# Product matmuls and gate matmuls in turn, in a gated MLP on one Trainium2 core

## The chip, the core and the metric

The kernel runs on one core of a Trainium2 chip (trn2). The time is that of the device for one execution, in microseconds; what is shown is the median of three runs. TensorE (PE, with its weight loads as PEld), VectorE (DVE), ScalarE (ACT), GpSimd (POOL) and the DMA queue of SyncE (SP) run side by side and wait for each other by semaphores.

## What is computed

Four sequences of 512 tokens with 256 features go through two residual layers. The first is a 256x256 layer whose weights are mixed per sequence out of eight matrices. The second is a gated MLP: a shared one, and the best two of eight experts for the sequence.

```
def _gemma_mlp(x, gate_w, up_w, down_w):
    g = jnp.einsum('bsh,hi->bsi', x, gate_w)
    u = jnp.einsum('bsh,hi->bsi', x, up_w)
    return jnp.einsum('bsi,ih->bsh', jax.nn.gelu(g, approximate=True) * u, down_w)
...
x = x + _L0_cond_ref(x, cond_8, L0_cond_weight, L0_cond_mask, L0_cond_bias)
x = x + _L1_cond_ref(x, cond_8, ...)
```

## The kernel before, in words

Tokens lie along the free axis, features on the partitions. A sequence is a "batch" of 24 steps, eight for the shared MLP and eight for each of its two experts. Step s makes 128 of the hidden features for all 512 tokens: a **gate** projection into g_ps, an **up** projection into u_ps (two halves, used in turn), gelu on ACT (L740), the product h of both on DVE (L995 or L1000), and a **down** projection that accumulates over the steps. Every operand of a matmul is split into a rounded part (hi) and a rest (lo), and each product of matrices is three products of parts. Gate and up are thus six matmuls of 512 columns each (`project`, L501 to L509; matmuls at L504, L505, L508).

The down projection has two forms. In batch 0, and for the last four steps of the last batch, it is plain: six matmuls of 512 columns (L556, or L605 by halves). Elsewhere (`fast`) two steps make a pair p, and Winograd's variant of Strassen's method multiplies a 2x2 of blocks with seven products in place of eight. The right-hand blocks are halves of h of 256 tokens (B11, B21, B22) and sums of them (T1 to T4, formed by DVE, split by ACT and DVE); the left-hand ones are blocks of the down weights and sums S1 to S4. Each product is three matmuls of 256 columns (`product`, L561 to L564; matmul L563). After the even step of a pair come P1, P2 and P3 (nine matmuls, `products_123`), after the odd one P6, P7, P4 and P5 (twelve, `products_4567`). P1, P6 and P7 lie in p_ps, the others in o_ps, both in PSUM. The order on PE is written out by hand, with LAG = 2:

```
for s in range(STEPS):
    if s + LAG < STEPS:
        gate_up(b, s + LAG)
    ...
    down(b, s)
```

so PE runs gate(s+2), up(s+2), down(s), gate(s+3), and so on. Batches 1 and 2 are one loop on every engine. Twice in a batch six matmuls of the next batch's first layer follow a down (L463).

What PE waits for: a gate waits for the gelu before it to have read g_ps, and for the lo part of its weights (POOL, L1193); the gate of step 0 for the parts of the new x1 as well (POOL, L1244). A down waits for h_lo. ACT takes its work in a fixed order: gelu of a step (L740); after an even one the copy of T (L767) and, once DVE has h, that of B11 (L754), which waits until all nine matmuls of the pair before are done (`down_done`), then b12 (L757); after an odd one the copy of B21 and B22 (L762). Weight splits (L711, L720, L722) come between. At a batch's end ACT also empties the PSUM of the products (L772, L773 once P1 to P3 are through, L777, L778 once P4 to P7 are) before the next gelu.

Of the kernel before, what the change touches and what calls it, by code (L numbers as in the profile page):

```python
# [35 lines left out]
def build(nc, xT, cond, l0_w, l0_mask, experts, shared, outT):  # L36
# [22 lines left out]
    with ExitStack() as ctx:  # L59
# [6 lines left out]
        def sem(name):  # L66
            return ctx.enter_context(nc.semaphore(name))
# [118 lines left out]
        t_done = sem("t_done")  # L186
        t_hi_done = sem("t_hi_done")
        t_lo_done = sem("t_lo_done")
        down_done = sem("down_done")
        sum0_done = sem("sum0_done")  # L190
        evac_done = sem("evac_done")
# [19 lines left out]
        def at_first(b):  # L211
            return isinstance(b, int) and b == 0
# [47 lines left out]
        def pair_count(b, p):  # L260

            return NP * (b - 1) + p
# [158 lines left out]
        def _(pe):  # L421
# [54 lines left out]
            def block_of(w, i):  # L476
                return w[:, i * P:(i + 1) * P]

            def half_of(h, i):
                return h[:, i * TH:(i + 1) * TH]  # L480
# [30 lines left out]
            def gate_up(b, s):  # L511
                n = STEPS * b + s
                w_hi, w_lo = gu_weights(s)
# [12 lines left out]
                pe.wait_ge(gelu_done, n)  # L526
                project(g_ps, w_hi, w_lo, GATE, b).then_inc(g_done, 1)
                if by_parts:
                    pe.wait_ge(gu_hi_done, s + 1)
                    pe.wait_ge(gu_lo_done, s + 1)  # L530
                if s < 2 and not at_first(b):
                    was_fast = not (isinstance(b, int) and b == 1)
                else:
                    was_fast = fast(b, s // 2 - 1)
                if was_fast and s % 2:
                    pe.wait_ge(t_done, 4 * pair_count(b, s // 2 - 1) + 4)
                elif not isinstance(n, int) or n >= 2:
                    pe.wait_ge(h_lo_done, n - 1)
                project(u_ps[:, s % 2], w_hi, w_lo, UP, b).then_inc(u_done, 1)
# [18 lines left out]
                        mm.then_inc(sum0_done, 1)  # L558
                mm.then_inc(down_done, 1)

            def product(ps, wt, ht, blk, hf, first, last):  # L561
                for i, (w, h) in enumerate(((0, 0), (0, 1), (1, 0))):
                    mm = pe.matmul(ps, block_of(wt[w], blk), half_of((h_hi, h_lo)[h], hf), start=(first and i == 0), stop=(last and i == 2))  # L563
                return mm  # L564

            def products_123(b, p):
                wait_d(b, p)
                pe.wait_ge(h_lo_done, STEPS * b + 2 * p + 2)
                if p == 0:
                    pe.wait_ge(x1_done, HH)  # L570
                    pe.wait_ge(out_done, 1)
                    pe.wait_ge(evac_done, 4 * b)
                first, last = p == 0, p == (LAST_FAST - 1 if at_last(b) else NP - 1)
                wt = d_weights(p)
                product(P1, wt, None, A11, B11, first, last)
                product(P2, wt, None, A12, B21, first, False)
                product(P3, wt, None, S4, B22, False, last).then_inc(down_done, 1)

            def products_4567(b, p):
                pe.wait_ge(t_lo_done, pair_count(b, p) + 1)  # L580
                if p == 0:
                    pe.wait_ge(out_done, HH)
                    pe.wait_ge(evac_done, 4 * b + 2)
                    if not (isinstance(b, int) and b == 1):
                        pe.wait_ge(x1_p4_done, b - 1)
                first, last = p == 0, p == (LAST_FAST - 1 if at_last(b) else NP - 1)
                wt = d_weights(p)
                product(P6, wt, None, S2, T2, first, False)
                product(P7, wt, None, S3, T3, False, last)
                product(P4, wt, None, A22, T4, first, False)  # L590
                product(P5, wt, None, S1, T1, False, last).then_inc(down_done, 1)

            def final_down(s):
                wh, wl = d_weights(s // 2)
# [11 lines left out]
                    if s == STEPS - 1:  # L606
                        mm.then_inc(final_done, 1)

            def down(b, s):
                if fast(b, s // 2):  # L610
                    if s % 2 == 0:
                        products_123(b, s // 2)
                    else:
                        products_4567(b, s // 2)
                elif at_first(b):
                    plain_down(b, s, [o_ps[:, oh] for oh in range(HH)], s == 0, s == STEPS - 1)
                elif s < STEPS - FINAL:
                    pe.wait_ge(x1_done, HH * B)
                    pe.wait_ge(rest_done, 1)
                    plain_down(b, s, LAST_PS, True, True)  # L620
                else:
                    final_down(s)

            def batch(b, with_next):
                for s in range(STEPS):
                    if s + LAG < STEPS:
                        gate_up(b, s + LAG)
                    elif with_next:
                        gate_up(b + 1, s + LAG - STEPS)
                    down(b, s)  # L630
                    if with_next and s == 13:
                        first_layer(b + 1, 0)
                    if with_next and s == 16:
                        first_layer(b + 1, 1)


            def keep_warm(count):
                for _ in range(count):
# [16 lines left out]
                    keep_warm(1)  # L655
            first_layer_0()
            first_gate_up()
            gate_up(0, 1)
            batch(0, True)
            with pe.Fori(1, B - 1) as b:  # L660
                batch(b, True)
# [3 lines left out]
        def _(act):  # L665
# [84 lines left out]
            def split_b11(b, p):  # L750
                n = STEPS * b + 2 * p
                act.wait_ge(h_done, n + 1)
                act.wait_ge(down_done, n - 1)
                act.copy(h_hi[:, 0:TH], u_ps[:, 0, 0:TH]).then_inc(h_hi_done, 1)  # L754
                if not (isinstance(b, int) and b == 1 and p == 0):
                    act.wait_ge(t_done, 4 * pair_count(b, p))
                act.copy(b12[:], u_ps[:, 0, TH:T]).then_inc(b12_done, 1)  # L757

            def split_b2(b, p):
                n = STEPS * b + 2 * p + 1  # L760
                act.wait_ge(h_done, n + 1)
                act.copy(h_hi[:, B21 * TH:(B22 + 1) * TH], u_ps[:, 1]).then_inc(h_hi_done, 1)  # L762

            def split_t(b, p):
# [595 lines left out]
```

## Time and profile before

| | |
|---|---|
| median of 3 runs | 416.71 us (415.83 to 416.97) |
| profiled execution | 416.73 us |
| its span (first to last instruction) | 414.9 us |
| PE busy | 409.4 us, 2133 matmuls |
| PE weight loads busy | 350.6 us, 2133 loads |
| DVE, ACT, POOL busy | 262.1, 234.7, 256.7 us |
| DMA | 36.24 MB, mean 87 GB/s |

A matmul's row in the profile starts where it starts streaming, and its length includes the way through the array, so that rows of neighbouring matmuls overlap. What a matmul costs is the distance from its start to the next one's. A row "x2" merges two instructions. "Idle before" counts only time in which the engine had nothing at all.

### The profile page before, as it was taken

To read this page: it belongs to the slowest core of one execution; us is meant where nothing else is said; L and a number is where in the kernel's file an instruction comes from. 1 tells how busy PE (TensorE), PEld (TensorE's weight loads), DVE (VectorE), ACT (ScalarE), POOL (GpSimd) and SP (SyncE) were. 2 spreads that over 40 slices of the span, in tenths; PEclk is the share of its full clock that TensorE was granted. 3 is DMA by queue.
4 is the path that set the end of the run, shared out by engine and by line. 5 is a ranking of instruction groups with operands and counts; after the bars stand their busy time and mean duration, and the time that the engine had idled before them with its cause. 6 is when DMAs were issued, how large, how long until landed. Compare 5 with 4: busy or idle time off the path is not lost.

```text
span 414.9 us, 7010 instructions
## 1 busy us (share of the span) xinstructions
PE 409.4 (99%) x2133; PEld 350.6 (85%) x2133; DVE 262.1 (63%) x452; ACT 234.7 (57%) x448; POOL 256.7 (62%) x275
## 2 busy tenths in 40 slices
PE   8999999999999999999999999999999999999997
PEld 5688888888888888888888888888888888888886
DVE  3556644244348877865767878775666675666684
ACT  5665454463425567665556566666465555766541
POOL 1565465378702459988533878998560885878630
DMA  7764324334200442243110053322300033222101
GB/s 241 244 199 108 96 81 126 98 102 104 76 25 9 122 126 76 77 134 96 42 38 0 25 177 90 112 76 76 101 25 25 0 117 87 78 92 87 40 12 51
DMA packets 20187, 36.24 MB, mean 87 GB/s; under 512 B 2242, under 2 KB 3010, under 8 KB 20162
## 3 DMA queue, kind: packets, MB, share of 16 engines
q1 hardware_dynamic: 19872, 35.66, 28.5%
q8 instruction: 13, 0.21, 0.2%
q10 hardware_dynamic: 290, 0.26, 0.2%
q14 instruction: 12, 0.10, 0.1%
HBM read 33.82 MB, written 2.10 MB: 87 GB/s over the span
## 4 chain that ended last, share of the span: by engine, by line
PE 96%; DMA 1%; DVE 1%; SPq 1%; issue 0%; ACT 0%; DVEq 0%
PE o_ps L563 12%; PE g_ps L505 11%; PE g_ps L504 11%; PE g_ps L508 10%; PE u_ps L505 10%; PE u_ps L508 10%; PE u_ps L504 10%; PE p_ps L563 9%; PE o_ps L556 8%; PE l_ps L463 2%; DMA l_raw<-l_w 1%; PE p_ps L444 1%; DVE t_raw L941 0%; PE o_ps L605 0%; SPq L276 0%
## 5 line engine op out<-in xcount | busy, mean ns | idle before, releaser
L1193 POOL TENSOR_TENSOR eg_lo<-raw_g,eg_hi 128x512 fp32r<-128x512 f32 x64 | 85.8, 1356 | 41.2 <-ACT eg_hi L711 41.2
L1000 DVE SCALAR_TENSOR_TENSOR u_ps<-gelu,route_cur,u_ps 128x512 f32<-128x512 f32 x64 | 48.3, 754 | 77.0 <-PE u_ps L508 77.0
L740 ACT ACTIVATE gelu<-g_ps 128x512 f32<-128x512 f32 x96 | 57.7, 601 | 59.7 <-PE g_ps L508 59.1
L505 PE MATMUL g_ps<-x_hi,eg_lo 128*128 128x512 f32 (+1 forms) x128 | 50.4, 394 | 0.0
L504 PE MATMUL g_ps<-x_hi,eg_hi 128*128 128x512 f32 (+1 forms) x128 | 50.1, 392 | 0.0
L505 PE MATMUL u_ps<-x_hi,eg_lo 128*128 128x512 f32 (+1 forms) x128 | 49.8, 389 | 0.0
L504 PE MATMUL u_ps<-x_hi,eg_hi 128*128 128x512 f32 (+1 forms) x128 | 49.8, 389 | 0.0
L762 ACT CAST h_hi<-u_ps 128x512 fp32r<-128x512 f32 x34 | 19.9, 587 | 49.8 <-DVE u_ps L1000 31.1
L1036 DVE TENSOR_TENSOR h_lo<-t_raw,h_hi 128x1024 fp32r<-128x1024 f32 x34 | 47.3, 1392 | 0.0
L995 DVE TENSOR_TENSOR u_ps<-gelu,u_ps 128x512 f32<-128x512 f32 x32 | 22.3, 696 | 31.2 <-PE u_ps L508 30.2
L1232 POOL TENSOR_TENSOR ed_lo<-raw_d,ed_hi 128x384 fp32r<-128x384 f32 x22 | 22.4, 1020 | 30.2 <-ACT ed_hi L720 30.2
L508 PE MATMUL g_ps<-x_lo,eg_hi 128*128 128x512 f32 (+1 forms) x128 | 39.6, 390 | 0.0
L508 PE MATMUL u_ps<-x_lo,eg_hi 128*128 128x512 f32 (+1 forms) x128 | 39.4, 389 | 0.0
L711 ACT CAST eg_hi<-raw_g 128x512 fp32r<-128x512 f32 x64 | 37.2, 621 | 0.0
L767 ACT CAST h_hi<-t_raw 128x1024 fp32r<-128x1024 f32 x34 | 35.6, 1048 | 0.3
L1031 DVE TENSOR_TENSOR h_lo<-u_ps,h_hi 128x512 fp32r<-128x512 f32 x34 | 23.5, 691 | 17.0 <-ACT h_hi L762 17.0
L754 ACT CAST h_hi<-u_ps 128x256 fp32r<-128x256 f32 x34 | 12.7, 373 | 32.9 <-PE o_ps L563 30.8
L1236 POOL TENSOR_TENSOR ed_lo<-raw_d,ed_hi 128x512 fp32r<-128x512 f32 x10 | 13.9, 1394 | 27.1 <-ACT ed_hi L724 27.1
L508 PEld LDWEIGHTS g_ps<-x_lo,eg_hi 128*128 128x128 f32 x128 | 24.0, 188 | 5.3
L504 PEld LDWEIGHTS u_ps<-x_hi,eg_hi 128*128 128x128 f32 x128 | 24.0, 188 | 5.2
L1234 POOL TENSOR_TENSOR ed_lo<-s_raw,ed_hi 128x512 fp32r<-128x512 f32 x22 | 28.4, 1290 | 0.0
L505 PEld LDWEIGHTS u_ps<-x_hi,eg_lo 128*128 128x128 f32 x128 | 24.0, 188 | 5.0
(234 smaller groups left out, 1120.6 us busy)
## 6 DMA issues: line engine op xcount, KB each, us to landing
raw_g<-experts SPq DMA_DIRECT2D x64, 256.0 KB, 2.8
raw_d<-experts SPq DMA_DIRECT2D x32, 256.0 KB, 2.8
l_raw<-l_w SPq DMA_DIRECT2D x8, 256.0 KB, 5.7
x_in<-xT SPq DMA_DIRECT2D x8, 256.0 KB, 4.4
raw_g<-shared SPq DMA_DIRECT2D x8, 256.0 KB, 4.4
raw_d<-shared SPq DMA_DIRECT2D x8, 256.0 KB, 2.9
outT<-out_sb SPq DMA_DIRECT2D x6, 256.0 KB, 3.2
mask<-l_mask SPq DMA_DIRECT2D x2, 128.5 KB, 6.0
```

Of the source, the lines that this page charges most:

```text
L504: pe.matmul(ps, w_hi[:, at:at + P], x1_at(x1_hi, b, hh), start=(hh == 0), stop=False)
L505: pe.matmul(ps, w_lo[:, at:at + P], x1_at(x1_hi, b, hh), start=False, stop=False)
L508: mm = pe.matmul(ps, w_hi[:, at:at + P], x1_at(x1_lo, b, hh), start=False, stop=(hh == HH - 1))
L556: mm = pe.matmul(psums[oh], block_of(w, blk), x, start=(first and i == 0), stop=(last and i == 2))
L563: mm = pe.matmul(ps, block_of(wt[w], blk), half_of((h_hi, h_lo)[h], hf), start=(first and i == 0), stop=(last and i == 2))
L711: act.copy(eg_hi[:, j % RING], raw_g[:, j % RAW_G]).then_inc(gu_hi_done, 1)
L740: act.activation(gelu[:, s % 2], g_ps[:], ACT.Gelu_apprx_tanh).then_inc(gelu_done, 1)
L767: act.copy(h_hi[:, T1 * TH:7 * TH], t_raw[:]).then_inc(t_hi_done, 1)
L1000: dve.scalar_tensor_tensor(u_ps[:, s % 2], gelu[:, s % 2], route_cur[:, k:k + 1], u_ps[:, s % 2], ALU.mult, ALU.mult).then_inc(h_done, 1)
L1036: dve.tensor_tensor(h_lo[:, at], t_raw[:], h_hi[:, at].bitcast(F32), ALU.subtract).then_inc(t_lo_done, 1)
L1193: pool.tensor_tensor(eg_lo[:, j % RING], raw_g[:, j % RAW_G], eg_hi[:, j % RING].bitcast(F32), ALU.subtract).then_inc(gu_lo_done, 1)
L1234: pool.tensor_tensor(ed_lo[:, q % RING_D, S1 * P:7 * P], s_raw[:], ed_hi[:, q % RING_D, S1 * P:7 * P].bitcast(F32), ALU.subtract).then_inc ...
```

## The change

PE's order is rotated: a step is now up(s+2), then down(s) with gate(s+3) laid into it. Gate matmuls, each for itself, alternate with the product matmuls of `fast` pairs; where the down is plain, the gate follows it as before. The matmuls are the same, 2133 of them. In the even step P1's three come first, then the waits of the gate, then gate and product in turn; in the odd step the gate's waits come after four products. P1's last matmul counts a new semaphore, `b11_read`, and ACT's copy of B11 waits for that (its three readers) and no longer for P2 and P3. The copy of B21 and B22 gets the wait that it had through B11's: `down_done` at n - 2.

```
             def up(b, s):
...
-            def products_123(b, p):
+            def products_123_and_gate(b, p, nb, ns):
+
                 wait_d(b, p)
                 pe.wait_ge(h_lo_done, STEPS * b + 2 * p + 2)
...
-                product(P1, wt, None, A11, B11, first, last)
-                product(P2, wt, None, A12, B21, first, False)
-                product(P3, wt, None, S4, B22, False, last).then_inc(down_done, 1)
...
+                product(P1, wt, A11, B11, first, last).then_inc(b11_read, 1)
+                wait_gate(nb, ns)
+                gate_part(nb, ns, 0)
+                product_part(P2, wt, A12, B21, 0, first, False)
+                gate_part(nb, ns, 1)
+                product_part(P2, wt, A12, B21, 1, first, False)
+                gate_part(nb, ns, 2)
+                product_part(P2, wt, A12, B21, 2, first, False)
+                gate_part(nb, ns, 3)
+                product_part(P3, wt, S4, B22, 0, False, last)
+                gate_part(nb, ns, 4)
+                product_part(P3, wt, S4, B22, 1, False, last)
+                product_part(P3, wt, S4, B22, 2, False, last).then_inc(down_done, 1)
+                gate_part(nb, ns, 5).then_inc(g_done, 1)
...
-                product(P6, wt, None, S2, T2, first, False)
-                product(P7, wt, None, S3, T3, False, last)
-                product(P4, wt, None, A22, T4, first, False)
-                product(P5, wt, None, S1, T1, False, last).then_inc(down_done, 1)
+                product(P6, wt, S2, T2, first, False)
+                product_part(P7, wt, S3, T3, 0, False, last)
+                wait_gate(nb, ns)
+                gate_part(nb, ns, 0)
+                product_part(P7, wt, S3, T3, 1, False, last)
+                product_part(P7, wt, S3, T3, 2, False, last)
+                gate_part(nb, ns, 1)
+                product_part(P4, wt, A22, T4, 0, first, False)
+                product_part(P4, wt, A22, T4, 1, first, False)
+                gate_part(nb, ns, 2)
+                product_part(P4, wt, A22, T4, 2, first, False)
+                product_part(P5, wt, S1, T1, 0, False, last)
+                gate_part(nb, ns, 3)
+                product_part(P5, wt, S1, T1, 1, False, last)
+                gate_part(nb, ns, 4)
+                product_part(P5, wt, S1, T1, 2, False, last).then_inc(down_done, 1)
+                gate_part(nb, ns, 5).then_inc(g_done, 1)
...
             def batch(b, with_next):
                 for s in range(STEPS):
                     if s + LAG < STEPS:
-                        gate_up(b, s + LAG)
+                        up(b, s + LAG)
                     elif with_next:
-                        gate_up(b + 1, s + LAG - STEPS)
-                    down(b, s)
+                        up(b + 1, s + LAG - STEPS)
+                    if s + LAG + 1 < STEPS:
+                        down_and_gate(b, s, b, s + LAG + 1)
+                    elif with_next:
+                        down_and_gate(b, s, b + 1, s + LAG + 1 - STEPS)
+                    else:
+                        down_and_gate(b, s, None, None)
...
             def split_b11(b, p):
                 n = STEPS * b + 2 * p
                 act.wait_ge(h_done, n + 1)
-                act.wait_ge(down_done, n - 1)
+                if p == 0:
+                    act.wait_ge(down_done, n - 1)
+                else:
+                    act.wait_ge(b11_read, pair_count(b, p))
...
             def split_b2(b, p):
                 n = STEPS * b + 2 * p + 1
                 act.wait_ge(h_done, n + 1)
+                act.wait_ge(down_done, n - 2)
```

PE in the loop over batches, before: a down of an even step, between the up of one step and the gate of the next. The weights are sd_hi and sd_lo for the down, sg_hi and sg_lo for gate and up.

```order
L508 MATMUL u_ps<-x_lo,sg_hi 128x512 x2
L563 MATMUL p_ps<-h_hi,sd_hi 128x256
L563 MATMUL p_ps<-h_lo,sd_hi 128x256
L563 MATMUL p_ps<-h_hi,sd_lo 128x256
L563 MATMUL o_ps<-h_hi,sd_hi 128x256
L563 MATMUL o_ps<-h_lo,sd_hi 128x256
L563 MATMUL o_ps<-h_hi,sd_lo 128x256
```

Three more o_ps matmuls and the six of the gate follow. The same place in the changed kernel:

```order
L579 MATMUL p_ps<-h_hi,sd_hi 128x256
L579 MATMUL p_ps<-h_lo,sd_hi 128x256
L579 MATMUL p_ps<-h_hi,sd_lo 128x256
L525 REGISTER_ALU
L533 MATMUL g_ps<-x_hi,sg_hi 128x512
L579 MATMUL o_ps<-h_hi,sd_hi 128x256
L533 MATMUL g_ps<-x_hi,sg_lo 128x512
L579 MATMUL o_ps<-h_lo,sd_hi 128x256
L533 MATMUL g_ps<-x_hi,sg_hi 128x512
L579 MATMUL o_ps<-h_hi,sd_lo 128x256
```

The gate's matmuls stand between those of P2 and P3, and the register instruction of the gate's wait stands in the middle of the down instead of behind it.

ACT in the loop, before: the copies of T and B11, and the work behind them.

```order
L767 CAST h_hi<-t_raw 128x1024 [waits down_done,t_done]
L754 CAST h_hi<-u_ps 128x256 [waits down_done,h_done]
L756 ISA
L757 COPY b<-u_ps 128x256 [waits t_done]
L716 ISA
```

And in the changed kernel:

```order
L826 CAST h_hi<-t_raw 128x1024 [waits down_done,t_done]
L811 REGISTER_ALU [waits h_done]
L812 CAST h_hi<-u_ps 128x256 [waits b11_read]
L814 REGISTER_ALU
L815 COPY b<-u_ps 128x256 [waits t_done]
```

Nothing moves on ACT; the copy of B11 waits for b11_read in place of down_done.

## Rows read from the trace of the kernel before

**Rows 1.** The page: span and busy time by engine.
```profile
span 414.9 us, 7010 instructions
...
PE 409.4 (99%) x2133; PEld 350.6 (85%) x2133; DVE 262.1 (63%) x452; ACT 234.7 (57%) x448; POOL 256.7 (62%) x275
```
**Rows 2.** The page: chain that ended last, by engine.
```profile
PE 96%; DMA 1%; DVE 1%; SPq 1%; issue 0%; ACT 0%; DVEq 0%
```
**Rows 3.** Timeline of PE, batch 1 (start us, length us, engine, line, operation): even step, odd down.
```profile
200.68 0.28 PE L563 MATMUL p_ps<-h_hi,ed_hi 128*128 128x256 f32 x1
200.79 0.28 PE L563 MATMUL p_ps<-h_lo,ed_hi 128*128 128x256 f32 x1
...
201.75 0.40 PE L504 MATMUL g_ps<-x_hi,eg_hi 128*128 x1
201.99 0.40 PE L505 MATMUL g_ps<-x_hi,eg_lo 128*128 x1
202.22 0.39 PE L504 MATMUL g_ps<-x_hi,eg_hi 128*128 x1
...
203.14 0.39 PE L504 MATMUL u_ps<-x_hi,eg_hi 128*128 x1
...
204.50 0.28 PE L563 MATMUL p_ps<-h_hi,ed_hi 128*128 128x256 f32 x1
204.61 0.28 PE L563 MATMUL p_ps<-h_lo,ed_hi 128*128 128x256 f32 x1
204.73 0.28 PE L563 MATMUL p_ps<-h_hi,ed_lo 128*128 128x256 f32 x1
...
205.93 0.40 PE L504 MATMUL g_ps<-x_hi,eg_hi 128*128 x1
```
**Rows 4.** Timeline of PE, batch 0: gate, up and plain down.
```profile
67.20 0.39 PE L504 MATMUL g_ps<-x_hi,eg_hi 128*128 128x512 f32 x1
...
68.56 0.39 PE L504 MATMUL u_ps<-x_hi,eg_hi 128*128 128x512 f32 x1
...
71.28 0.39 PE L504 MATMUL g_ps<-x_hi,eg_hi 128*128 128x512 f32 x1
```
**Rows 5.** Timeline of PE weight loads, at the second product block of Rows 3.
```profile
204.50 0.19 PEld L563 LDWEIGHTS p_ps<-h_lo,ed_hi 128*128 128x128 f32 x1
204.62 0.19 PEld L563 LDWEIGHTS p_ps<-h_hi,ed_lo 128*128 128x128 f32 x1
```
**Rows 6.** Line L563: length in ns min/median/max of the first product matmul and the next.
```profile
L563 PE MATMUL p_ps<-h_hi,ed_hi x66: 277/278/284, 158.0 to 399.6; 128*128 128x256 f32 x66
...
L563 PE MATMUL p_ps<-h_lo,ed_hi x66: 282/283/284, 158.1 to 399.7; 128*128 128x256 f32 x66
...
L563 PE MATMUL p_ps<-h_hi,sd_hi x36: 277/278/381, 125.9 to 351.6; 128*128 128x256 f32 x36
```
**Rows 7.** Who waited for whom: PE's longest since batch 0, and ACT's before L754.
```profile
PE g_ps L504 <- ACT gelu L740: 0.3, 1, 0.3
ACT h_hi L754 <- PE o_ps L563: 30.8, 33, 1.2
```
**Rows 8.** Timelines of ACT and PE: gelu of step 9 and gate 10, batch 1.
```profile
153.28 0.61 ACT L740 ACTIVATE gelu<-g_ps 128x512 f32<-128x512 f32 x1
155.21 0.40 PE L504 MATMUL g_ps<-x_hi,eg_hi 128*128 x1
```
**Rows 9.** Timeline of ACT at the end of batch 1.
```profile
218.49 0.39 ACT L772 COPY x_in<-p_ps 128x256 f32<-128x256 f32 x1
218.75 0.62 ACT L773 COPY s_raw<-o_ps 128x512 f32<-128x512 f32 x1
219.34 0.60 ACT L740 ACTIVATE gelu<-g_ps 128x512 f32<-128x512 f32 x1
```
**Rows 10.** Timelines of POOL and PE: lo weights of gates 8 and 9, gate 8, batch 3.
```profile
332.74 3.54 POOL L1193 TENSOR_TENSOR eg_lo<-raw_g,eg_hi 128x512 fp32r<-128x512 f32 x2
344.65 0.40 PE L504 MATMUL g_ps<-x_hi,eg_hi 128*128 128x512 f32 x1
```

More of the change, by code:

```diff
@@ L188, in build @@
         t_lo_done = sem("t_lo_done")
+        b11_read = sem("b11_read")
         down_done = sem("down_done")
@@ L509, in project, with wait_gate @@
                 return mm
-            def gate_up(b, s):
-                n = STEPS * b + s
-                w_hi, w_lo = gu_weights(s)
+            def wait_gate(b, s):
                 by_parts = at_first(b) and s < FIRST
@@ L525, in gate_up, with gate_part, gate, up @@
                     pe.wait_ge(x1_lo_done, HH * b + HH)
-                pe.wait_ge(gelu_done, n)
-                project(g_ps, w_hi, w_lo, GATE, b).then_inc(g_done, 1)
-                if by_parts:
+                pe.wait_ge(gelu_done, STEPS * b + s)
+            def gate_part(b, s, i):
+                w_hi, w_lo = gu_weights(s)
+                hh = i // 2 if i < 4 else i - 4
+                w, x = (w_lo if i in (1, 3) else w_hi), (x1_hi if i < 4 else x1_lo)
+                at = GATE + hh * P
+                return pe.matmul(g_ps, w[:, at:at + P], x1_at(x, b, hh), start=(i == 0), stop=(i == 5))
+            def gate(b, s):
+                wait_gate(b, s)
+                for i in range(6):
+                    mm = gate_part(b, s, i)
+                mm.then_inc(g_done, 1)
+            def up(b, s):
+                n = STEPS * b + s
+                w_hi, w_lo = gu_weights(s)
+                if at_first(b) and s < FIRST:
                     pe.wait_ge(gu_hi_done, s + 1)
@@ L559, in plain_down, with product_part, product @@
                 mm.then_inc(down_done, 1)
-            def product(ps, wt, ht, blk, hf, first, last):
-                for i, (w, h) in enumerate(((0, 0), (0, 1), (1, 0))):
-                    mm = pe.matmul(ps, block_of(wt[w], blk), half_of((h_hi, h_lo)[h], hf), start=(first and i == 0), stop=(last and i == 2))
+            def product_part(ps, wt, blk, hf, i, first, last):
+                w, h = ((0, 0), (0, 1), (1, 0))[i]
+                return pe.matmul(ps, block_of(wt[w], blk), half_of((h_hi, h_lo)[h], hf), start=(first and i == 0), stop=(last and i == 2))
+            def product(ps, wt, blk, hf, first, last):
+                for i in range(3):
+                    mm = product_part(ps, wt, blk, hf, i, first, last)
                 return mm
-            def products_123(b, p):
+            def products_123_and_gate(b, p, nb, ns):
                 wait_d(b, p)
@@ L574, in products_123, with products_4567_and_gate @@
                 wt = d_weights(p)
-                product(P1, wt, None, A11, B11, first, last)
-                product(P2, wt, None, A12, B21, first, False)
-                product(P3, wt, None, S4, B22, False, last).then_inc(down_done, 1)
-            def products_4567(b, p):
+                product(P1, wt, A11, B11, first, last).then_inc(b11_read, 1)
[12 more added lines that the diff above has]
+                gate_part(nb, ns, 5).then_inc(g_done, 1)
+            def products_4567_and_gate(b, p, nb, ns):
                 pe.wait_ge(t_lo_done, pair_count(b, p) + 1)
@@ L607, in final_down, with down_and_gate @@
                         mm.then_inc(final_done, 1)
-            def down(b, s):
+            def down_and_gate(b, s, nb, ns):
                 if fast(b, s // 2):
                     if s % 2 == 0:
-                        products_123(b, s // 2)
+                        products_123_and_gate(b, s // 2, nb, ns)
                     else:
-                        products_4567(b, s // 2)
-                elif at_first(b):
+                        products_4567_and_gate(b, s // 2, nb, ns)
+                    return
+                if at_first(b):
                     plain_down(b, s, [o_ps[:, oh] for oh in range(HH)], s == 0, s == STEPS - 1)
@@ L622, in down @@
                     final_down(s)
+                if ns is not None:
+                    gate(nb, ns)
             def batch(b, with_next):
@@ L657, in _ @@
             first_gate_up()
-            gate_up(0, 1)
+            gate(0, 1)
+            up(0, 1)
+            gate(0, 2)
             batch(0, True)
```

## The prediction

> **What bounds the kernel now.** I read the page first. PE is busy 409.4 of 414.9 us [rows 1], and the chain that ended last is PE for 96% [rows 2]; the list of waits has PE idle for 0.3 us at most once the first gate has run [rows 7]. So no wait is worth anything by itself: the time is the number of matmuls times the distance from one start to the next. The timelines of PE give that distance, and it isn't the same everywhere.
>
> - **512 columns behind 512.** Batch 0 has nothing else: eighteen matmuls from gate to gate in 71.28 - 67.20 = 4.08 us [rows 4], 0.227 each. Six are 1.36 us.
> - **256 columns in a block.** Nine products and the first gate matmul: 201.75 - 200.68 = 1.07. Eight of the distances, from 200.79 on, are 0.96, so 0.120 each, and the first is 0.11. Twelve: 205.93 - 204.50 = 1.43, of which the first is again 0.11 [rows 3]. The record of the first product is 278 ns long, of the second 283, in p_ps at every one of some hundred places [rows 6]. I take 0.113 for a product that stands directly behind a 512, 0.120 for one behind another product.
> - **512 behind a block.** The six gate matmuls after nine products take 203.14 - 201.75 = 1.39, the up behind them 204.50 - 203.14 = 1.36 [rows 3], and in batch 0 gate is 1.36 as well [rows 4]. A block leaves 0.03 us to be paid by those that follow it, the first two most (0.24 and 0.23).
>
> Every load starts at the start of the matmul before its own: loads at 204.50, 204.62 [rows 5] against matmuls at 204.50 and 204.61 [rows 3]. So one load is under way per matmul and no more. Behind a 512 it has 0.227 us; in a block load follows load at 0.12, and its 0.19 us reach past the start of the matmul that uses it. The clock granted was 2.4 GHz, at which 256 columns alone are 0.107 us.
>
> **The change, part by part.** Its worth is counted over `fast` steps: p_ps's first matmuls number 66 + 36 = 102 at L563 [rows 6], three a pair, so 34 pairs, 68 steps.
>
> *Products between gate matmuls.* Nothing is added to or taken from PE's matmuls; only neighbours change. Even step: behind an up or a gate matmul stand P1's first, three of P2, P3's first and P3's second, six at 0.113; three stay behind a product. Before, one was short and eight long. Five more are shorter by 0.007, that is 0.035 us. Odd step: P6's first, P7's second, P4's first and third, P5's second and third are short, six again, where it was one: 0.035. Together 68 x 0.035 = 2.4 us.
>
> *The debt of a block.* 0.03 for 68 steps is 2.0 us in all. It may vanish, since no run of more than four products is left; or stay, since the gate's first matmul still stands behind three or four products, and nine leave the same debt as twelve would, so its size doesn't grow with the block. The trace has no shorter block. The ends are 2.0 us gained and nothing; below nothing, it may be paid again after every product, which is the third rival. I take nothing: the nearest row, a gate matmul behind a product, is the 0.24 at 201.75 [rows 3].
>
> *Loads of the page.* The Trainium skill (TensorE: Matmul & The Clock Gate, LDWEIGHTS and Back-to-back issue gap) gives a load of 128 columns as 128 / 1.2, 107 ns, and a matmul as N / 2.4 + 2.5, 109 ns at 256. By it a load fits under a 256 as it does under a 512, a block costs nothing, and the sum would be zero. The 0.120 in place of 0.109 speaks against that, the equally unexplained 0.227 in place of 0.216 for it.
>
> *The gate's waits, moved forward.* They stand six products (0.72 us) earlier in the even step, eight (0.96) in the odd one, and now hold up products too. The gelu that gate 10 needs ended at 153.28 + 0.61 = 153.89, the gate began at 155.21 [rows 8]: 1.32 of slack, 0.36 after the move. Weights are no matter: those of gate 8 and 9 of batch 3 were there at 332.74 + 3.54 = 336.28, eight us before the gate at 344.65 [rows 10]. The register instruction in front of the wait stands in the middle of products; before, it stood behind twelve of them, and the distance to the gate was still 0.12. Nothing for all of it, by that cover.
>
> *Later ends of the downs.* P3 and P5 now end just before the gate does, some 1.1 us later against the gelu. Behind them on ACT is only the emptying of PSUM at a batch's end: 218.49 to 219.34, 0.85 us, and then the gelu, 0.60 [rows 9]. The gelu would end some 1.25 us after its gate; the next gate begins 1.36 (up) less 0.16 (the tail of the gate's record) plus 0.35 or 0.47 (products) after it, 1.55 or more. About 0.3 us are left, four times in the run. Nothing, again.
>
> *ACT's copy of B11.* ACT waited 30.8 us in 33 places for the products [rows 7], 0.93 each, with nobody behind it that held PE up. Left with `down_done` it would wait longer now; with `b11_read` it is free about a gate earlier. No time of its own, but it is what keeps ACT in step.
>
> **Sum.** 2.4 us less. Made against the profiled execution, 416.73 us (span 414.9 and 1.8 around it), which is the median of 416.71 too: **414.3 us**, 0.6% faster.
>
> **Rivals.**
> 1. *The debt goes as well.* 2.4 + 2.0 = 4.4 us: 412.3. For it: the first gate in batch 0, behind 512s, has no debt at all [rows 4], and with a 512 after every one or two products loads are never behind for long. Against it: the block of three or four.
> 2. *No gain.* What a short product saves, the next gate matmul gives back: the 0.007 at the head of a block would be a shift in when a record starts and no time. Five returned a step, 0.035, leave 416.7. For it: 0.24 for the first gate matmul is more than 0.007 over 0.227. It is also what the page's figures give. Against: the debt is 0.03 a block, not 0.007.
> 3. *Slower: the debt is paid after every product.* Each gate matmul stays at 0.235, as the first ones behind a block [rows 3], none recovers between products, the products find no head start and stay at 0.120, and the 0.03 moves on into the up. Even step with up: 9 x 0.12 + 6 x 0.235 + 1.39 = 3.88, before 1.07 + 1.39 + 1.36 = 3.82. 0.06 a step, 4.1 us: 420.8. It decides from where the gate and up matmuls of a step average over 0.232 with short products (3.82 less 1.038, by twelve).
> 4. *The gate finds gelu late.* The 0.3 and 0.36 us above hold only if ACT isn't later than by my count. 0.3 late at a dozen steps with the least slack is 3.6 us and eats the gain: about 418.
>
> **How the numbers follow.** Forecast 0.38, debt gone 0.28, no gain 0.19, slower by the debt 0.12, gelu late 0.03. What can be told from no change is 0.3%, 1.25 us. Forecast and first rival are beyond it: faster 0.66. No gain is within: same 0.19. The other two: slower 0.15. The range starts below the first rival, at 412.0, takes in no gain and part of the fourth, and ends at 417.4; the third is left out.
>
> **What would show it.** Products directly behind a gate matmul at 0.11 to the next start, gate matmuls between them at 0.227 to 0.24, the six distances of gate together some 1.39 (1.36: first rival; 1.41: third). A pair of steps (even 1.07, odd 1.43, and twice 1.39 + 1.36) 7.93 us where it is 8.00. No row in PE's waits for gelu over 0.1 us, and ACT's wait for L563 before the copy of B11 gone or far below 30.8 us. Wrong would be: PE waiting in the middle of a down, or gate matmuls that on average are over 0.235.

## The result, and the profile after

The changed kernel takes 418.45 us in the median (418.25 to 418.96, five runs), the kernel before 416.62 in the same comparison: a ratio of 1.005, 95% interval 1.0037 to 1.0064. It is slower by 0.5%, 1.8 us; forecast were 414.3 us and at most 417.4. The profiled execution took 418.25 us.

The page of the changed kernel: span, busy time, the chain that ended last by engine.

```profile
span 416.2 us, 7042 instructions
...
PE 411.3 (99%) x2133; PEld 350.8 (84%) x2133; DVE 263.4 (63%) x452; ACT 235.5 (57%) x448; POOL 256.3 (62%) x275
...
PE 94%; DVE 2%; DMA 1%; issue 1%; SPq 1%; ACT 1%; DVEq 0%
```

Against [rows 1, 2], PE is busy 1.9 us longer with the same 2133 matmuls. The chain that ended last is still PE, for 94%. Part of the loss is in what a matmul costs, part in waits. The timeline of PE in the changed kernel (start, length, engine, line, operation) shows where, in the even step that answers to the first block of [rows 3]:

```profile
200.28 0.28 PE L579 MATMUL p_ps<-h_hi,ed_hi 128*128 128x256 f32 x1
200.39 0.28 PE L579 MATMUL p_ps<-h_lo,ed_hi 128*128 128x256 f32 x1
...
200.63 0.40 PE L533 MATMUL g_ps<-x_hi,eg_hi 128*128 x1
200.86 0.28 PE L579 MATMUL o_ps<-h_hi,ed_hi 128*128 128x256 f32 x1
200.98 0.40 PE L533 MATMUL g_ps<-x_hi,eg_lo 128*128 x1
201.22 0.28 PE L579 MATMUL o_ps<-h_lo,ed_hi 128*128 128x256 f32 x1
201.34 0.40 PE L533 MATMUL g_ps<-x_hi,eg_hi 128*128 x1
201.58 0.28 PE L579 MATMUL o_ps<-h_hi,ed_lo 128*128 128x256 f32 x1
201.69 0.40 PE L533 MATMUL g_ps<-x_hi,eg_lo 128*128 x1
201.92 0.28 PE L579 MATMUL o_ps<-h_hi,ed_hi 128*128 128x256 f32 x1
202.04 0.40 PE L533 MATMUL g_ps<-x_lo,eg_hi 128*128 x1
...
202.52 0.40 PE L533 MATMUL g_ps<-x_lo,eg_hi 128*128 x1
202.76 0.40 PE L505 MATMUL u_ps<-x_hi,eg_hi 128*128 x1
...
204.12 0.28 PE L579 MATMUL p_ps<-h_hi,ed_hi 128*128 128x256 f32 x1
...
208.32 0.28 PE L579 MATMUL p_ps<-h_hi,ed_hi 128*128 128x256 f32 x1
```

The six gate distances are 0.23, 0.24, 0.24, 0.23, 0.24, 0.24, together 1.42 us where they were 1.39; the nine product distances are the rest of 202.76 - 200.28 = 2.48, so 1.06 where they were 1.07. Of the five products behind a gate matmul four take 0.12 to the next start and one (201.58) 0.11. A pair of steps is 208.32 - 200.28 = 8.04, before 8.00 (3.82 + 4.18). Over 34 pairs that is 1.36 us.

Two other losses are plain waits. The timelines of PE and of ACT at the start of batch 2:

```profile
220.56 0.28 PE L579 MATMUL p_ps<-h_hi,ed_hi 128*128 128x256 f32 x1
220.77 0.50 PE L533 MATMUL g_ps<-x_hi,sg_hi 128*128 x1
221.11 0.28 PE L579 MATMUL p_ps<-h_lo,ed_hi 128*128 128x256 f32 x1
```
```profile
218.80 0.37 ACT L812 CAST h_hi<-u_ps 128x256 fp32r<-128x256 f32 x1 [2.07 <-PE o_ps L579]
...
219.33 0.39 ACT L831 COPY x_in<-p_ps 128x256 f32<-128x256 f32 x1
...
220.08 0.64 ACT L795 ACTIVATE gelu<-g_ps 128x512 f32<-128x512 f32 x1
```

The gelu ends at 220.72 and the gate begins at 220.77; the two distances 0.21 and 0.34 stand for 0.12 and 0.23, and the step is 0.17 us longer. Ahead of that gelu ACT has not only the emptying of PSUM but the copies of B11 and b12, for B11's copy of a batch's *first* pair still waits for `down_done` and sat 2.07 us. The same happens at the start of batch 3: 0.33 us together. And the timeline of PE at the end:

```profile
411.18 0.28 PE L650 MATMUL g_ps<-l_hi,ed_lo 128*128 128x256 f32 x1
411.63 0.35 PE L650 MATMUL o_ps<-x_hi,ed_hi 128*128 128x256 f32 x1 [0.18 <-DVE x_lo L1065]
```

0.45 us where 0.12 is usual: 0.33 us for DVE, which sums the products behind the last fast pair, and got them late. In all 1.36 + 0.33 + 0.33 = 2.0 us, against 1.8 measured. The spans are only 1.3 us apart because the first gate began at different times, 19.48 us before and 18.75 after. From there to the start of the last matmul (411.67 and 413.01) it is 392.19 and 394.26, 2.1 us more, which fits the sum.

### The profile page after: what moved, and what is told of

Its sections match the earlier page's. It is cut to its first block, busy times and chain, and to the rows that moved or that the text cites. A ratio compares the mean times of both kernels' runs of the same rounds, so it can differ in the third digit from the quotient of the medians.

```text
span 416.2 us, 7042 instructions
## 1 busy us (share of the span) xinstructions
PE 411.3 (99%) x2133; PEld 350.8 (84%) x2133; DVE 263.4 (63%) x452; ACT 235.5 (57%) x448; POOL 256.3 (62%) x275
## 4 chain that ended last, share of the span: by engine, by line
PE 94%; DVE 2%; DMA 1%; issue 1%; SPq 1%; ACT 1%; DVEq 0%
PE g_ps L533 32%; PE o_ps L579 12%; PE u_ps L505 10%; PE u_ps L509 10%; PE u_ps L506 10%; PE p_ps L579 9%; PE o_ps L572 8%; PE l_ps L464 2%; DMA l_raw<-l_w 1%; PE p_ps L445 1%; DVE t_raw L1000 0%; SPq L277 0%; DVE u_ps L1059 0%; DVE out_sb L1144 0%; DVE x_lo L1065 0%
## 5 line engine op out<-in xcount | busy, mean ns | idle before, releaser
L1095 DVE TENSOR_TENSOR h_lo<-t_raw,h_hi 128x1024 fp32r<-128x1024 f32 x34 | 48.5, 1428 | 0.0
L533 PE MATMUL g_ps<-x_lo,eg_hi 128*128 128x512 f32 (+1 forms) x128 | 46.6, 395 | 0.0
L1291 POOL TENSOR_TENSOR ed_lo<-raw_d,ed_hi 128x384 fp32r<-128x384 f32 x22 | 24.1, 1093 | 30.6 <-ACT ed_hi L775 30.4
L509 PEld LDWEIGHTS u_ps<-x_lo,eg_hi 128*128 128x128 f32 x128 | 24.0, 188 | 5.0
```

The source lines that it names most:

```text
L533: return pe.matmul(g_ps, w[:, at:at + P], x1_at(x, b, hh), start=(i == 0), stop=(i == 5))
L1095: dve.tensor_tensor(h_lo[:, at], t_raw[:], h_hi[:, at].bitcast(F32), ALU.subtract).then_inc(t_lo_done, 1)
```

## The experiments

There are fourteen kernels. The table has those that settle what unequal lengths cost, each with a pair of steps in its profile (from one P1 to the next). The timeline resolves a hundredth of a microsecond, the time some tenths of a per cent. A *return* is a place where a matmul of 512 columns stands behind one of 256.

| kernel | a pair, us | returns from 256 to 512 columns in a pair | time, ratio to before |
|---|---|---|---|
| before | 8.00 | 2 | 1 |
| the change | 8.04 | 12 | 1.005 |
| e2 waits alone | 8.00 | 2 | 0.9997 |
| e10 gate in one piece | 8.04 | 4 | one run, 418.07 us |
| e11 two products a gate in even steps | 8.03 | 10 | one run, 417.77 us |
| e12 one product within up | 8.01 | 3 | one run, 417.65 us |
| e13, e14 one block of 21 | 7.98 | 1 | 1.0023, 1.0006 |

### The two parts of the change, and the two waits

**e1_b11_batch_start.**

```
             def split_b11(b, p):
-                if p == 0:
+                if isinstance(b, int) and b == 1 and p == 0:
                     act.wait_ge(down_done, n - 1)
```

> The changed kernel, with the copy of B11 of a batch's first pair (batches 2 and 3) also waiting for b11_read in place of down_done. Theory 1 (three separate costs in the profile of the change: 0.04 us in each of 34 pairs on PE, 0.165 us in front of the gate of step 3 at two batch starts, about 0.34 us in the last six steps): the two 0.165 us go, PE's distance at the first gate matmul of step 3 falls from 0.34 to 0.23, the pairs stay at 8.04 us; 0.33 us less than the change, 1.0035 to 1.0045 of before. Rival (ACT is late there because of emptying PSUM, not of the B11 copy): the 0.165 us stay and so does the time.

418.63 us, 1.0052 (1.0039 to 1.0064). The wait is gone, in the timeline of PE at the same place:

```profile
220.75 0.40 PE L533 MATMUL g_ps<-x_hi,sg_hi 128*128 x1
220.98 0.28 PE L579 MATMUL p_ps<-h_lo,ed_hi 128*128 128x256 f32 x1
```

and pairs stay at 8.04. The time doesn't show it: 0.33 us is a third of what the interval covers (1.0 us). The cause of the wait is shown, its 0.33 us in the profile alone.

**e2_wait_only.** The kernel before with the semaphores of the change, and `b11_read` for every pair but the very first:

```
-                product(P1, wt, None, A11, B11, first, last)
+                product(P1, wt, None, A11, B11, first, last).then_inc(b11_read, 1)
...
-                act.wait_ge(down_done, n - 1)
+                if isinstance(b, int) and b == 1 and p == 0:
+                    act.wait_ge(down_done, n - 1)
+                else:
+                    act.wait_ge(b11_read, pair_count(b, p))
```

> The kernel before with the new waits alone (b11_read for the copy of B11, down_done for that of B21 and B22), PE's order as before. Theory 1: PE waits for nothing there, so no difference: 1.000 of before, pairs at 8.00 us; ACT's 30.8 us of waiting in front of the B11 copy fall to under 20 us. Rival (the earlier copy of B11 collides with PE's reads or delays DVE): 0.04 us a pair, 1.003 or more.

416.64 us, 0.9997 (0.9988 to 1.0006), every pair 8.00. In front of the copy of B11 (L758 here) ACT waits 14.9 us in 22 places and 7.3 in 11 for DVE's product, 22.2 us instead of 30.8 for PE; the expected "under 20" is missed. It is idle time either way.

**e3_interleave_only.** The change, with B11 as before:

```
-                if p == 0:
-                    act.wait_ge(down_done, n - 1)
-                else:
-                    act.wait_ge(b11_read, pair_count(b, p))
+                act.wait_ge(down_done, n - 1)
```

> The changed kernel with the copy of B11 waiting for down_done as before, so the interleaving alone. Theory 1: the downs end 0.2 us before the gate does, so the B11 copy, b12 and on even steps from 8 the two weight copies (0.27 + 0.26 + 0.42 + 0.5 us) stand between the gate and the next gelu; with gelu's 0.6 that is about 1.84 us after the gate, where 1.67 are to be had: some 0.2 us lost at eight steps a batch, 4 us in all over the change, about 1.013 of before. Rival (ACT has room enough and the second part of the change is idle): same as the change, 1.0045.

429.64 us in the median of three runs (428.99 to 429.94), 1.0316 (1.0298 to 1.0334): 13 us over before, where 5 or 6 were expected. A fourth run took 1052.61 us, for a reason that isn't known, and is left out. PE was dry for 6.2 us before 21 gates, waiting for gelu. ACT's timeline at a step with a split of x:

```profile
160.83 0.37 ACT L809 CAST h_hi<-u_ps 128x256 fp32r<-128x256 f32 x1 [2.05 <-PE o_ps L579]
...
162.82 0.61 ACT L795 ACTIVATE gelu<-g_ps 128x512 f32<-128x512 f32 x1
```

The direction and the mechanism hold: two microseconds of copies between the end of the down and the gelu. The size was off, because at steps 8 and 10 the split of x stands there as well (the gate 0.95 us behind the product ahead of it), and because a late gate costs more than the delay of its gelu. Without that split, as at the gate of 171.94, the distance to the gate is 0.43 in place of 0.12 and the one behind it 0.34 in place of 0.23: 0.4 us, where 0.2 were expected. So the second part of the change isn't idle. It takes back some 11 us that the first would cost.

**e4_last_step_block.** e1, with the last fast step as before:

```
+                    elif at_last(b) and s == 2 * LAST_FAST - 1:
+                        products_4567(b, s // 2)
+                        gate(nb, ns)
```

> As e1_b11_batch_start, with the products of the last fast step in one block and gate 22 behind them, as in the kernel before. Theory 1: the sums of the products that DVE does at the end start 1.1 us earlier against the gate and the wait of 0.34 us in front of the last step's products goes: 0.3 us less than e1, about 1.003 of before, and what is left is the 0.04 us a pair (1.36 us, 1.0033). Rival (the wait at the end has another cause, the later gelu): no difference from e1.

417.98 us, 1.0031 (1.0019 to 1.0043), as expected (1.003); behind the start of batch 1 no distance over 0.25 us is left in its profile. With both waits gone, what remains is the 0.04 us a pair.

### What the unequal lengths cost

**e5_plain_alternate.** Batch 0's six down matmuls, all of 512 columns, in turn with the gate's.

```
+                        mm = pe.matmul(o_ps[:, oh], block_of(w, blk), x, ...)
...
+                        gm = gate_part(nb, ns, k)
```

> The changed kernel, and in batch 0 the six plain down matmuls of 512 columns (o_ps) alternate with the six of the gate (g_ps), 512 beside 512. Theory A (it is the unequal length that costs: a 512 behind a 256 takes 0.233 to 0.241 us to the next start): all distances in batch 0 stay at 0.227 and a step at 4.08 us. Theory B (it is the change of the PSUM tile or of the moving operand from one matmul to the next): distances of 0.233 or more in batch 0, a step of 4.12 us or more.

Theory A holds. PE in batch 0, from a down matmul to that of the next step:

```profile
62.29 0.39 PE L587 MATMUL o_ps<-h_hi,ed_hi 128*128 128x512 f32 x1
...
66.37 0.39 PE L587 MATMUL o_ps<-h_hi,ed_hi 128*128 128x512 f32 x1
```

4.08 us, 0.227 for each of eighteen. Neither the change of PSUM tile nor that of the moving operand costs anything. (Its one time, 419.5 against 417.08, isn't used: its first gate begins at 19.83, 1.1 us later than in the change.)

**e6_block_192 and e7_interleaved_192.** 192 columns in each product matmul, in blocks and interleaved:

```
-                    mm = pe.matmul(ps, block_of(wt[w], blk), half_of((h_hi, h_lo)[h], hf), ...)
+                    mm = pe.matmul(ps[:, 0:192], block_of(wt[w], blk), half_of((h_hi, h_lo)[h], hf)[:, 0:192], ...)
```

> The kernel before with product matmuls of 192 columns in place of 256, in blocks; the last 64 tokens of each half are left out of the products. Theory A (a product in a block is held at 0.12 us by its weight load, one load at a time): distances stay at 0.12 us, the time falls by nothing to speak of, and the 0.03 us debt of a block stays or grows. Theory B (0.12 is 256 columns at 2.4 GHz plus 0.013): 192 columns take 0.080 + 0.013, 0.093 us, 714 products give 19 us less.

> The changed kernel with product matmuls of 192 columns; the last 64 tokens of each half are left out of the products. Theory A (load bound): a product directly behind a gate matmul still takes 0.11 to 0.12 us to the next start, since the gate's load needs that; the gate matmuls behind take more than 0.24 us; not faster than e6. Theory B (length bound): products 0.093, gate matmuls as in the change, 0.233 to 0.241.

410.76 and 413.55 us in one run each, against 417.08 before: 6.3 and 3.5 less, not 19. PE and its loads in e6's block, then PE in e7:

```profile
195.01 0.28 PE L563 MATMUL p_ps<-h_hi,ed_lo 128*128 128x192 f32 x1
195.12 0.27 PE L563 MATMUL p_ps<-h_hi,ed_hi 128*128 128x192 f32 x1
...
196.12 0.41 PE L504 MATMUL g_ps<-x_hi,eg_hi 128*128 x1
```
```profile
195.03 0.19 PEld L563 LDWEIGHTS p_ps<-h_hi,ed_hi 128*128 128x128 f32 x1
195.14 0.19 PEld L563 LDWEIGHTS p_ps<-h_lo,ed_hi 128*128 128x128 f32 x1
```
```profile
200.17 0.25 PE L579 MATMUL o_ps<-h_hi,ed_hi 128*128 128x192 f32 x1
200.25 0.42 PE L533 MATMUL g_ps<-x_hi,eg_lo 128*128 x1
200.51 0.25 PE L579 MATMUL o_ps<-h_lo,ed_hi 128*128 128x192 f32 x1
```

In the block, loads and matmuls are 0.11 us apart, though interleaved products of this length show 0.08: this fits a bound by the load, and shorter products bring little. Interleaved, a product takes 0.08 to the next start, but the gate matmul behind it 0.26: together 0.34, as much as 0.11 and 0.227 apart. What the short product gives, the long one behind it gives back. This is theory A for e6, with 0.11 in place of 0.12, and for e7 except that the product itself is short. At 256 columns the loads could be 0.11 us apart but are 0.12 [rows 5], so there the load alone doesn't bound.

**e8_block_bf16.** Products of the upper halves of the same words, read as bf16 at a stride of two:

```
+ block_of(wt[w], blk).bitcast(BF16)[:, 1:2*P:2], half_of((h_hi, h_lo)[h], hf).bitcast(BF16)[:, 1:2*TH:2]
```

> The kernel before with the product matmuls' operands read as the upper halves (bf16) of the same words, 128 and 256 elements at a stride of two, in blocks; the products are of lower precision. Theory A (the load of four-byte weights is what holds a block at 0.12 us): distances fall to 0.107 to 0.113 us and the gate behind the block is at 0.227, 1.36 us for six; 21 x 0.01 + 0.06 us a pair, 9 us less. Theory B (a fixed cost for each pair of load and matmul): 0.12 us stays, and the debt as well.

414.32 us in one run. PE from P6 to the up:

```profile
203.44 0.29 PE L564 MATMUL p_ps<-h_hi,ed_hi 128*128 128x256 bf16 x1
...
204.70 0.28 PE L564 MATMUL o_ps<-h_hi,ed_lo 128*128 128x256 bf16 x1
204.72 0.48 PE L505 MATMUL g_ps<-x_hi,eg_hi 128*128 x1
205.04 0.40 PE L506 MATMUL g_ps<-x_hi,eg_lo 128*128 x1
...
207.58 0.29 PE L564 MATMUL p_ps<-h_hi,ed_hi 128*128 128x256 bf16 x1
```

and its first load of the block:

```profile
203.44 0.10 PEld L564 LDWEIGHTS p_ps<-h_hi,ed_hi 128*128 128x128 bf16 x1 [0.26 <-issue]
```

Neither theory holds whole. Ten of the twelve distances are 0.113, so the four-byte operands do hold a product at 0.12; whether the stationary or the moving one does it, this run can't tell. The first is 0.13. The gate's first matmul is recorded 0.02 behind the last product and then takes 0.32, together what 0.11 and 0.23 make, so the two records have to be taken together. The step is 207.58 - 203.44 = 4.14 us where it was 4.18, and twelve times 0.007 alone would give 0.08. So a block costs more here, 0.06 us in place of 0.02 (4.14 less 12 x 0.113 and 12 x 0.227). The debt is larger, not gone. The whole is 2.8 us less, not 9.

### Counting the returns

**e10_gate_in_one_piece.** On e4; the gate stands whole behind P1, or behind the first four products:

```
                 product(P1, wt, A11, B11, first, last).then_inc(b11_read, 1)
+                gate(nb, ns)
+                product(P2, wt, A12, B21, first, False)
+                product(P3, wt, S4, B22, False, last).then_inc(down_done, 1)
```

> As e4_last_step_block, but the gate laid in as one piece of six (even step: three products, gate, six products, up; odd step: four, gate, eight, up). Theory 1 (a cost for each return from products to 512): two returns of 0.02 us a step in place of one, even step 3.84, odd 4.20, a pair 8.04, the same as the full interleaving. Rival (only alternation one by one costs; long pieces are free): 8.00 as before.

```profile
201.12 0.40 PE L533 MATMUL g_ps<-x_hi,eg_hi 128*128 x1
...
202.51 0.28 PE L579 MATMUL o_ps<-h_hi,ed_hi 128*128 128x256 f32 x1
...
203.22 0.40 PE L505 MATMUL u_ps<-x_hi,eg_hi 128*128 x1
...
204.61 0.28 PE L579 MATMUL p_ps<-h_hi,ed_hi 128*128 128x256 f32 x1
```

The pair is 8.04 us (200.77 to 208.81). The gate behind three products takes 202.51 - 201.12 = 1.39, the up behind six 204.61 - 203.22 = 1.39: four returns in place of two cost 0.04 us, 0.02 each, with no single alternation at all. The rival falls.

**e11_two_products_a_gate.** On e4; in even steps `gate, product, product` three times, then three gate matmuls.

> As e4_last_step_block, but in even steps two products follow each of the first three gate matmuls and the last three gate matmuls are in a row: four returns from products to 512 in place of six. Theory 1: an even step loses 0.005 to 0.008 us for each return, 3.83 to 3.84, against 3.845 in the change and 3.82 before. Rival (the position of single products decides): no difference from e4, 3.845.

The pair is 8.03 us, between before and the change, as theory 1 has it. Seven pairs, from 208.92 to 265.11, are 56.19 us, 8.027 each, so ten returns cost 0.027 over before.

**e12_single_in_up.** On e2; P1's first matmul stands alone behind the up's third:

```
                     pe.matmul(ps, w_hi[:, at:at + P], x1_at(x1_hi, b, hh), start=(hh == 0), stop=False)
+                    if hh == 1 and between:
+                        between()
```

> The kernel e2_wait_only with the first product matmul of P1 (256 columns) standing alone between the third and fourth matmul of the up in front of it. Theory 1 (a 256 leaves the following 512 a distance of 0.233 or more even when it stands alone): the product 0.113, the 512 behind it 0.233, so together 0.346 as 0.120 + 0.227, even step 3.82 to 3.83. Rival (a single product behind several 512s costs 0.113 and leaves no debt): the 512 behind it 0.227, even step 3.81.

```profile
200.55 0.28 PE L576 MATMUL p_ps<-h_hi,ed_hi 128*128 128x256 f32 x1
200.66 0.40 PE L508 MATMUL u_ps<-x_hi,eg_lo 128*128 x1
...
201.36 0.28 PE L583 MATMUL p_ps<-h_lo,ed_hi 128*128 128x256 f32 x1
```

The plainest case of the question. The product itself takes 0.11, then the three matmuls of 512 columns behind it 201.36 - 200.66 = 0.70 where three are 0.68. So it gained 0.007 and lost nearly 0.02; the pair is 8.01. One single product behind 512s already leaves a debt, if a smaller one than a block that is followed by a whole gate.

**e9_one_block_of_21, e13_block_of_21_gelu_first, e14_block_of_21_tidied.** The law turned round: both downs of a pair behind each other, one return a pair. On e2:

```
+                    if fast(b, s // 2):
+                        if s % 2:
+                            down(b, s - 1)
+                            down(b, s)
+                    else:
+                        down(b, s)
```

> The kernel e2_wait_only with the two downs of a fast pair behind each other (up, nine products, twelve products, gate), so one block of 21 products a pair in place of two. Theory 1 (each return from products to 512 columns costs 0.02 us net, 0.027 paid by the matmuls behind less 0.007 at the head of the block, whatever the block's length): a pair takes 7.98 where it was 8.00, 34 x 0.02 = 0.7 us less, 0.998 of before, if ACT's next gelu is in time (B11, b12, weight copies and gelu behind P1, some 2.4 us, against 2.5 us of products). Rival (the debt grows with the length of the block): 8.00 or more. Second rival (gelu late at steps with x splits): PE stalls there, slower than before.

430.33 us, 1.0323 (1.0309 to 1.0337): PE stalls for late gelus, as the second rival has it, but before some 35 gates and not only at steps with splits of x. PE in batch 1:

```profile
164.99 0.50 PE L505 MATMUL g_ps<-x_hi,eg_hi 128*128 x1 [0.53 <-ACT gelu L746]
```

The gelu of the odd step stands on ACT behind the copy of B11, which now waits for a P1 that comes a gate and an up later. e13 puts that gelu ahead of the copy:

```
+                if not (s % 2 and fast(b, s // 2)):
+                    activate(b, s)
...
+                if s % 2 == 0 and fast(b, s // 2):
+                    activate(b, s + 1)
```

> As e9_one_block_of_21, with ACT's gelu of the odd step moved in front of the copy of B11, so that it no longer stands behind a copy that waits for the first three products. Theory 1 (a return from products to 512 columns costs 0.02 us, and e9's time was lost to late gelus alone): pairs of 7.98 us, no wait of PE for gelu over 0.1 us in the loop, 0.7 us less than before, 0.998. Rival (the gate of an odd step, which now follows its up directly, still finds gelu late because of the copies and splits ACT has ahead of it): stalls of 0.3 to 0.8 us at some steps stay and eat the 0.7 us.

417.61 us, 1.0023 (1.0014 to 1.0032). Two P1, a pair apart:

```profile
195.42 0.28 PE L564 MATMUL p_ps<-h_hi,ed_hi 128*128 128x256 f32 x1
...
203.40 0.28 PE L564 MATMUL p_ps<-h_hi,ed_hi 128*128 128x256 f32 x1
```

7.98 us: a block of 21 leaves the same debt as one of nine, and one return fewer gives 0.02 back. Both expectations are met at once, for four late gelus and a wait at the end cost more than that. e14 mends three places: `pick_cond` at step 2 ahead of B11, the splits of x at steps 7 and 8, the last fast pair in two blocks.

> As e13_block_of_21_gelu_first, with the three places mended where it waited: the small copy of the mixing weights at step 2 stands on ACT before the copy of B11 and not behind it, the two splits of the next x stand at steps 7 and 8 in place of 8 and 10, and the last fast pair has its products in two blocks as before. Theory 1 (0.02 us for each return from products to 512 columns, nothing else): 33 pairs x 0.02 = 0.66 us less than before, 0.9984, no wait for gelu over 0.1 us. Rival (each mended wait only lets the next one show, or the 0.02 us come back elsewhere): 1.000 or more.

417.01 us, 1.0006 (0.9996 to 1.0015). The end is as before and the wait of step 5's gate is gone, but the gate of step 13 still waits some 0.2 us and that of step 9 now 0.3, in batches 1 and 2. That is the rival's first half. Five pairs of batch 3 stay at 8.00, and there the trace shows something new. PE at one of their gates, then its loads:

```profile
371.61 0.40 PE L505 MATMUL g_ps<-x_hi,eg_hi 128*128 128x512 f32 x1
...
372.99 0.39 PE L505 MATMUL u_ps<-x_hi,eg_hi 128*128 128x512 f32 x1
```
```profile
371.16 0.19 PEld L509 LDWEIGHTS u_ps<-x_lo,eg_hi 128*128 128x128 f32 x1
371.40 0.19 PEld L505 LDWEIGHTS g_ps<-x_hi,eg_hi 128*128 128x128 f32 x1
```

In these pairs the gelu ended 0.10 us or less ahead of the last matmul of the up (behind those that end 0.16 or more ahead nothing is lost), and the gate's load started late by 0.02 us (four times) or 0.07 (once): here 0.24 behind the load before it in place of 0.23. PE was never dry, and there are only 512s around, yet some 0.02 us are lost at each, here 372.99 - 371.61 = 1.38 for a gate of 1.36, with a first distance of 0.24, like that of a gate behind a block. The lateness of the load alone doesn't settle it, since the load of the gate at 347.62 was 0.05 late and cost nothing. Had all 33 pairs kept their 0.02 us the gain would be 0.7 us, less than the width of its interval (0.8). No version that computes the same result beat the kernel before.

## Why the prediction was wrong

**The bound** was read right: PE, by the number of matmuls times their distances, and no wait. The list of distances was right too; 0.227, 0.120, 0.113 and the debt of 0.03 us come back in every kernel whose blocks are of 256 columns in fp32r.

**Products between gate matmuls, 2.4 us, with the debt taken as nothing: the step that failed.** It took 0.113 for the worth of every product behind a 512 and let the debt stay as it was, one a step. Both halves were off. Of six products a step that were to take 0.113 two do (in the even step those at 200.28 and 201.58), so the nine are 1.06 and not 1.04. And the debt grew, where the sum had no change and its bounds only a gain of 2.0 us or nothing. Over a pair, by the starts in both timelines, the 21 products take 2.48 us where they took 2.51 (0.026 less; 0.07 less was forecast), and the 24 matmuls of 512 columns 5.56 where they took 5.49 (0.065 more; no change was forecast): in 34 pairs 0.9 us less and 2.2 more. The two terms together came to +1.4 us in place of -2.4, of the wrong sign.

The reason that they can't be booked apart is in e12: its lone product gained 0.007 and its three followers paid nearly 0.02. In fp32r a short distance at a block's head and long ones behind the block came together in every kernel. Counted by returns, the law reads: a pair of steps is 21 x 0.120 + 24 x 0.2267 = 7.96 us, and 0.02 net for each return that is followed by six or more matmuls of 512 columns, 7.98 with one (e13), 8.00 with two, 8.04 with four (e10). A return that is cut off by the next product costs less: 12 returns cost 0.04 over 2.

**The third rival** came true in its mechanism, the debt beginning anew behind each product, at a third of its price: 0.04 a pair for 0.12. Its gate, 1.41, was right (1.42); but the products kept a part of their short distances (1.06 and not 1.08), and the up behind them was 204.12 - 202.76 = 1.36, not 1.39. Its threshold fits: the gate and up matmuls of the even step average (1.42 + 1.36) / 12 = 0.232, right at it, and with products longer than its 1.038 the step is 3.84, over 3.82. It had a chance of 0.12, and the range left it out. The trace of before held the argument for more: a head start of 0.007 and a debt of 0.027 stood side by side 68 times, and the second is the larger.

**Loads.** The prediction's reading, that in a block load follows load and so holds the products, isn't enough at 256 columns, since e6 has loads 0.11 us apart. In bf16 the distance fell to 0.113, so part of the 0.120 is the four-byte operands. The Trainium skill (TensorE: Matmul & The Clock Gate, LDWEIGHTS) has a load of 128 columns at 107 ns; the 0.11 between loads in e6 are near it. The 109 ns that the Trainium skill's formula gives for a matmul of 256 columns (same page, Back-to-back issue gap) are there the gap of an isolated matmul; no block here reached them, not in bf16 either (0.113), and the measured distances decide.

**The gate's waits, moved forward:** right for the loop, no wait over 0.1 us there. **Later ends of the downs:** right for the loop, wrong for two places. The 0.3 us that were to be left at a batch's start forgot B11 and b12 in front of the emptying of PSUM, since for the first pair the wait is not the new one (e1). And the end of the run wasn't looked at: DVE's sums behind the last fast pair (e4). 0.33 us each.

**ACT's copy of B11:** right that it has no worth of its own (e2) and keeps ACT in step; how much, e3 shows: 11 us.

What stays open is why a 512 behind a 256 takes longer. Known is that it comes with unequal lengths and not with a change of the PSUM tile (e5), that one product is enough (e12) and 21 are no worse than nine (e13), and that products with loads of 0.10 us in bf16 leave it too (e8). Unequal length isn't the only way to it: a gate whose load came a little late cost 0.02 us too, among 512s alone (e14), and behind a stall for gelu the gate's later distances are 0.24 and 0.23 as well. A rival therefore stands untested, that both are a matter of the loads: the gate's were of four bytes and 0.19 us long in every kernel, and no run changed them by themselves. No run separates the moving operand's way into the array from the order in which instructions reach PE either.

## What to carry to other kernels

Two distances that deviate in opposite directions at the two ends of a block are one effect; book them together before making more ends. Here matmuls of unequal length were best in few long runs, and a run's length cost nothing; but a return is worth only 0.02 us, and one late gelu (0.2 us or more in e13 and e14) outweighs ten of them. When an order is rotated, check the first and last turn of the loop by themselves: there the waits are others, and both of this change's avoidable losses were there.

## What the runs showed of the hardware

- Start to start in a run of one length, with a load for each: 0.227 us for 512 columns fp32r, 0.120 for 256, 0.11 for 192 (e6); 256 in bf16 0.113 (e8).
- The first bf16 load behind fp32r matmuls was not started at the start of the matmul ahead of it but at that of its own (203.44), and its product took 0.13 us to the next start instead of 0.11 (e8). A block in another type cost 0.06 us where one in the same type costs 0.02.
- A return from 256 to 512 columns costs 0.02 us net (e10, e13): up to 0.01 us on each of the first matmuls of 512 columns, less the 0.007 at the head of the next block.
- A gelu that ended only 0.10 us ahead of the matmul before the gate that waits for it cost 0.02 us at that gate, though PE was never dry; 0.16 us ahead cost nothing, and neither did one case of 0.07 (e14).
